# Decoder layer on one core: four PSUM banks for the maximum pass and two for the transposed scores, in place of three and three

## The chip, the core and the metric

The kernel runs on one core of a Trainium2 chip. The metric is the device time of one execution in microseconds (us), lower is better. "Before" is the kernel as it stands, "after" the changed one; both compute the same output.

## What is computed

One decoder layer on x of shape (2, 2048, 512): causal self-attention with 16 heads of 32, cross-attention to a context of 77 rows, and a mixture of 8 experts of which each token uses 2, each followed by a residual addition and a layer norm. The change lies in the causal self-attention alone:

```python
qkv = x @ Wqkv.T
q, k, v = jnp.split(qkv, 3, axis=-1)          # 16 heads of 32
dots = jnp.einsum('bhid,bhjd->bhij', q, k) * scale
dots = jnp.where(causal_mask, -jnp.inf, dots)
attn = jax.nn.softmax(dots, axis=-1)
out = jnp.einsum('bhij,bhjd->bhid', attn, v)
...
x = _layernorm(x + _L0_attn_ref(x, ...))
```

## The kernel before

There are three stages in order of time: projections (`project`), self-attention (`self_attention`), and everything behind it (`second_half`). The self-attention works through 8 groups (2 batches, 4 groups of 4 heads). A group has 4 chunks c of 512 query positions. Chunk c is worked through in 4(c+1) key tiles kt of 128 positions, so a group has 40 tiles; a tile has one unit for each of the 4 heads, so there are 160 units in a group and 1280 in all (`VU`). The tiles with kt < 4c have the full 512 columns; the last four of a chunk lie on the diagonal and have 512, 384, 256 and 128 columns. Of the 40 tiles, 24 are full and 16 diagonal. In this text "tile 29" is the 29th of a group, counted from 0.

Each score is computed twice, in two streams that share TensorE:

- The **transposed scores** `st_ps`, one unit at a time (`scores`, L865, and L868 for the mask on the diagonal). ScalarE takes a unit's exponential into `probs` (L762). TensorE multiplies the probabilities with the values (`values`, L885, into the bank `o_ps`), four steps behind the tile's last unit. The row sums come from GpSimd, which adds tiles up in `total` (L637), and at every third full tile from TensorE (`sums`, L899, into the bank `den_ps`), six steps behind.
- The **maximum pass**, scores the other way round, `s_ps` (`aux`, L851), from which VectorE takes row maxima (L804 for full blocks, L807 and L808 for blocks with the diagonal). It runs ahead of the other stream, 160 blocks and 4 small transposes (kind "rows", L843, read at L745 and L797) for a group. The list `DONE` spreads them over the 160 steps.

The order of instructions on each engine is written out by `step(i, s, ...)`: TensorE's step s issues the transposed score of unit s, then one block of the maximum pass, then `values` if a tile is due (the fourth step of each tile), then `sums` (the second step of a tile), then `totals` of a finished chunk, then further blocks of the maximum pass if the step has more than one. Each engine goes through its own list in order and waits on semaphores.

PSUM has eight banks of 512 float32 per partition. The attention stage holds one each for `o_ps` and `den_ps` and divides the other six between the two streams. A unit's bank is `p % RING`, and before its matmul TensorE waits until the exponential of the unit RING before it is done:

```python
pe.wait_ge(exp_done.sem, exp_done.at(i, before(p, RING, 2 * NVU)))     # scores, transposed
...
pe.wait_ge(s_read.sem, s_read.at(i, before(n, RING, 2 * NAUX)))        # maximum pass
```

ScalarE has other work in its list, placed by steps: the eviction of `o_ps` (`o_raw`, L768) behind the first exponential of the second tile after a chunk, that of `den_ps` (L772) two tiles later, and the conversion `o_out` (L777) of a tile that GpSimd has scaled (`o_sb`, L647), 46 steps after the chunk.

Of the kernel before, what the change touches and what calls it, by code (L numbers as in the profile page):

```python
# [5 lines left out]
F32, F16, BF16 = mybir.dt.float32, mybir.dt.float16, mybir.dt.bfloat16  # L6
# [7 lines left out]
P = 128  # L14
# [3 lines left out]
CH = 512  # L18
NC = N // CH
CPB = T // CH  # L20
# [45 lines left out]
def stored_at(n):  # L66

    return 16 * n + 1
# [333 lines left out]
def self_attention(nc, S, x_rows, q_parts, k_parts, v_rows, o_parts, inv_rows):  # L402
# [23 lines left out]
    NKU, NVU, NAUX = len(KU), len(VU), len(AUX)  # L426
# [3 lines left out]
              for c in range(CPB)]  # L430
    ADDS = [n for tiles in POOLED for n in tiles[1:]]
    NP = 5
    RING = 3

    VALUES, SUMS = 4, 6
    TOTALS = 12
# [59 lines left out]
    def before(n, ring, per):  # L496

        k = n % per
        return n - ring if k >= ring else n - k - 1 - (per - 1 - k) % ring
# [18 lines left out]
    def unit_at(s, lag, first, end):  # L518

        p = s - lag  # L520
        return None if (first is not None and p < first) or (end is not None and p >= end) else p
# [13 lines left out]
    def aux_at(s, first, end):  # L535

        if first is not None:
            reached = [AHEAD + (done_by(TAIL) - AHEAD) * n // TAIL for n in (s, s + 1)]
        else:
            reached = done_by(s), done_by(s + 1)  # L540
        return [n for n in range(*reached) if end is None or n < 2 * NAUX]

    with ExitStack() as stack:
        sb = lambda *a: stack.enter_context(nc.sbuf_tensor(*a))
        ps = lambda *a: stack.enter_context(nc.psum_tensor(*a))
# [19 lines left out]
        o_sb = sb("o_sb", [P, CH], F32)  # L565
        o_out = sb("o_out", [P, 2, 2, CH], F16)
        st_ps = ps("st_ps", [P, RING, CH], F32)
        s_ps = ps("s_ps", [P, RING, CH], F32)
        o_ps = ps("o_ps", [P, CH], F32)
        den_ps = ps("den_ps", [P, CH], F32)  # L570
        made, const_ready, factors_ready = (stack.enter_context(nc.semaphore(s)) for s in
# [14 lines left out]
        s_read = Count(nc, stack, "s_read", 2 * NAUX)  # L586
# [144 lines left out]
        @block.scalar  # L731
        def _(act):
            exp_done.lead(act)
            o_taken.lead(act)
            den_taken.lead(act)
            o_hi_done.lead(act)
            upper_ready.lead(act)

            def upper(i, n):

                k = n // NAUX * CPB + AUX[n % NAUX][1]
                slot = n % (2 * NAUX) % RING
                act.wait_ge(s_ready.sem, s_ready.at(i, n))
                act.wait_ge(rows_moved[k % 2], stored_at(2 * (CPB * i + k // 2)))
                nc.scalar.activation(max_rows[:, k % 2, 0], s_ps[0:HG * TT, slot, 0:P], ACT.Copy,  # L745
                                     scale=-1.0 / QK).then_inc(upper_ready.sem, 1)

            def step(i, s, first, end):
                for n in aux_at(s, first, end):
                    if AUX[n % NAUX][0] == "rows":  # L750
                        upper(i, n)
                p = unit_at(s, 0, first, end)
                if p is not None:
                    c, kt, h = VU[p % NVU]
                    off = max(kt - c * TT, 0) * P
                    k = p // HG
                    act.wait_ge(st_ready.sem, st_ready.at(i, p))
                    if h == 0:

                        act.wait_ge(pv_done.sem, pv_done.at(i, k - NP))  # L760
                        act.wait_ge(added.sem, added.at(i, adds_upto(k - NP) - 1))
                    nc.scalar.activation(probs[:, k % NP, h, off:], st_ps[:, p % (2 * NVU) % RING, off:], ACT.Exp,  # L762
                                         scale=SCALE).then_inc(exp_done.sem, 1)
                c = chunk_at(s, TAKEN[0], first, end)
                if c is not None:
                    act.wait_ge(pv_done.sem, pv_done.at(i, c // CPB * NKU + LAST_TILE[c % CPB]))
                    act.wait_ge(scaled.sem, scaled.at(i, c - 2))
                    nc.scalar.activation(o_raw[:, c % 2], o_ps[:], ACT.Copy).then_inc(o_taken.sem, 1)  # L768
                c = chunk_at(s, TAKEN[1], first, end)
                if c is not None:  # L770
                    act.wait_ge(den_ready.sem, den_ready.at(i, c))
                    nc.scalar.activation(den[:, c % 2], den_ps[:], ACT.Copy, scale=1.0 / XS).then_inc(den_taken.sem, 1)  # L772
                c = chunk_at(s, UPPER, first, end)
                if c is not None:
                    act.wait_ge(scaled.sem, scaled.at(i, c))
                    act.wait_ge(o_stored[c % 2], stored_at(CPB * i + c // 2))
                    nc.scalar.activation(o_out[:, c % 2, 0], o_sb[:], ACT.Copy).then_inc(o_hi_done.sem, 1)  # L777

            for n in range(AHEAD):
                if AUX[n][0] == "rows":  # L780
                    upper(0, n)
            laps(act, step)

        @block.vector
        def _(dve):
            for count in (s_read, max_ready, recips):
                count.lead(dve)

            def aux(i, n):
                what, c, unit = AUX[n % NAUX]  # L790
                slot = n % (2 * NAUX) % RING
                k = n // NAUX * CPB + c
                dve.wait_ge(s_ready.sem, s_ready.at(i, n))
                if what == "rows":

                    dve.wait_ge(upper_ready.sem, upper_ready.at(i, k))
                    nc.vector.scalar_tensor_tensor(max_rows[:, k % 2, 1], s_ps[0:HG * TT, slot, 0:P], -1.0 / QK,  # L797
                                                   max_rows[:, k % 2, 0], ALU.mult,
                                                   ALU.subtract).then_inc(s_read.sem, 1)
                    return  # L800
                j, h, s = unit
                highest = seg_max[:, k % 2, h, j, s:s + 1]
                if s < c:
                    nc.vector.reduce_max(highest, s_ps[:, slot], AX.X).then_inc(s_read.sem, 1)  # L804
                else:
                    width = (j + 1) * P
                    nc.vector.memset(ticked[:, j * HG + h:j * HG + h + 1], 0.0)  # L807
                    nc.vector.tensor_tensor_reduce(s_ps[:, slot, 0:width], s_ps[:, slot, 0:width],  # L808
                                                   later[:, CH - width:CH], 1.0, MASKED, ALU.add, ALU.max,
                                                   highest).then_inc(s_read.sem, 1)  # L810
                if n % NAUX == LAST_MAX[c]:

                    dve.wait_ge(s_read.sem, s_read.at(i, n))
                    nc.vector.reduce_max(row_max[:], seg_max[:, k % 2, :, :, 0:c + 1], AX.X).then_inc(max_ready.sem, 1)

            def step(i, s, first, end):
                for n in aux_at(s, first, end):
                    aux(i, n)
                c = chunk_at(s, INVERTED, first, end)
                if c is not None:  # L820
                    dve.wait_ge(den_moved[c % 2], 16 * (CPB * i + c // 2 + 1))
                    nc.vector.reciprocal(inv_small[:, c % 2], inv_small[:, c % 2]).then_inc(recips.sem, 1)

            dve.wait_ge(made, 7)
            for n in range(AHEAD):
                aux(0, n)
            laps(dve, step)

        @block.tensor
        def _(pe):  # L830
# [3 lines left out]
            def aux(i, n):  # L834
                what, c, unit = AUX[n % NAUX]
                k = n // NAUX * CPB + c
                slot, a = n % (2 * NAUX) % RING, k // CPB % 2

                pe.wait_ge(s_read.sem, s_read.at(i, before(n, RING, 2 * NAUX)))
                if what == "rows":  # L840

                    pe.wait_ge(max_ready.sem, max_ready.at(i, k))
                    nc.tensor.transpose(s_ps[0:HG * TT, slot, 0:P], row_max[:].rearrange("p h j -> p (h j)"),  # L843
                                        ident_f[:]).then_inc(s_ready.sem, 1)
                    return
                j, h, s = unit
                if j == h == s == 0:

                    pe.wait_ge(qk_loaded[a][c], 6 * 16 * (i + k // (2 * CPB) + 1))
                width = CH if s < c else (j + 1) * P  # L850
                nc.tensor.matmul(s_ps[:, slot, 0:width], q_pair[a][0:NR, c, h, j * P:(j + 1) * P],  # L851
                                 k_pair[a][0:NR, h, s * CH:s * CH + width], start=True,
                                 stop=True).then_inc(s_ready.sem, 1)
# [78 lines left out]
            for n in range(AHEAD):  # L932
                aux(0, n)
# [670 lines left out]
```

## Time and profile before

| | |
|---|---|
| runs | 2633.06, 2633.9, 2635.76 us, median 2633.9 us |
| the profiled execution | 2630.97 us, its span 2629.2 us, mean granted clock 0.958 |
| busy over the span | TensorE 2430.0 us (92%), VectorE 1715.9 (65%), ScalarE 1097.3 (42%), GpSimd 1119.8 (43%) |
| attention stage | first transposed score at 303.9 us, last at 1333.2 us |

The page divides the span into 40 slices of 66 us; the attention stage is the fifth to the twentieth. A matmul's row shows its whole way through the array (0.38 us at 512 columns), and the next one can begin 0.22 us behind it. "Idle before" of weight loads (PEld) counts time in which matmuls run, so it is more than TensorE loses.

### The profile page before, as it was taken

Reading aid. Unit: us, or ns where it says so; the run is one execution under the profiler, and the core shown is the slowest. Engines: PE = TensorE matmul, PEld = TensorE weight load, DVE = VectorE, ACT = ScalarE, POOL = GpSimd, SP = SyncE. Lnnn points to the kernel's source line nnn. Section 1 sums busy time; section 2 is a strip of 40 time slices with the busy share of each in tenths; the row PEclk is TensorE's granted clock in tenths of the full one; section 3 lists DMA queues with packets and bytes.
Section 4 is the critical chain, followed back from the end, with each engine's and each line's share of the span. In section 5 each row is a group of like instructions: output and inputs, shape, how many; then the busy total and the mean of one; then the engine's idle time right before and its main releaser. Section 6 shows DMA issues by size and latency. Waiting matters only on the chain. (4 is left out here: it accounts for less than half of the span.)

```text
span 2629.2 us, 42902 instructions
## 1 busy us (share of the span) xinstructions
PE 2430.0 (92%) x13556; PEld 1018.3 (39%) x13556; DVE 1715.9 (65%) x3957; ACT 1097.3 (42%) x2066; POOL 1119.8 (43%) x404
## 2 busy tenths in 40 slices
PE   8999799999999999999956799999999999999998
PEld 3444223332333233323213354444445454454543
DVE  4443687776777677767405477767677776767665
ACT  4331256665666566666623242332324232322420
POOL 0000379988898989898952111102111111101100
PEclk9999799999999999999977899999999999999999
DMA  7864312212121212140021101010100101010000
GB/s 250 294 212 156 89 38 54 58 42 59 42 58 42 63 38 76 28 111 20 25 93 60 45 1 62 1 46 18 41 22 1 63 1 46 17 45 17 1 17 17
DMA packets 130506, 155.66 MB, mean 59 GB/s; under 512 B 19838, under 2 KB 98174, under 8 KB 129245
## 3 DMA queue, kind: packets, MB, share of 16 engines
q1 hardware_dynamic: 130269, 152.69, 18.9%
q8 instruction: 126, 2.06, 0.3%
q14 instruction: 111, 0.91, 0.1%
HBM read 99.96 MB, written 52.17 MB: 58 GB/s over the span
## 5 line engine op out<-in xcount | busy, mean ns | idle before, releaser
L762 ACT ACTIVATE probs<-st_ps 128x512 f32<-128x512 f32 (+3 forms) x1280 | 605.3, 536 | 359.0 <-PE st_ps L865 206.6
L637 POOL TENSOR_TENSOR total<-total,probs 128x2048 f32<-128x2048 f32 (+3 forms) x200 | 706.3, 3531 | 77.8 <-ACT probs L762 65.6
L804 DVE TENSOR_REDUCE seg_max<-s_ps 128x1 f32<-128x512 f32 x768 | 506.2, 684 | 143.4 <-PE s_ps L851 139.9
L865 PE MATMUL st_ps<-q_pair,k_pair 98*128 98x512 f16 (+3 forms) x1280 | 445.5, 362 | 36.6 <-ACT probs L762 22.7
L851 PE MATMUL s_ps<-k_pair,q_pair 96*128 96x512 f16 (+3 forms) x1280 | 446.0, 363 | 31.9 <-DMA q_pair<-q_parts 11.2
L1429 PE MATMUL fps<-x2T,w_p_hi 128*128 128x512 f16 x1024 | 317.3, 379 | 0.0
L885 PE MATMUL o_ps<-probs,v_sb 128*32 128x512 f32 (+3 forms) x2560 | 309.0, 556 | 0.0
L808 DVE CUSTOM_DVE_ANT_0 s_ps<-s_ps,later 128x384 f32<-128x384 f32 (+3 forms) x512 | 250.4, 497 | 89.1 <-issue 85.9
L1429 PE MATMUL fps<-w_p_hi,hT 128*128 128x512 f16 x1024 | 306.1, 381 | 0.0
L865 PEld LDWEIGHTS st_ps<-q_pair,k_pair 98*128 98x128 f16 x1280 | 124.8, 99 | 357.7 <-ACT probs L762 264.7
L1133 POOL TENSOR_TENSOR rstd<-rstd,keep_power 128x4 f32<-128x4 f32 x24 | 26.1, 1090 | 552.0 <-DVE rstd L1254 552.0
L1148 POOL TENSOR_TENSOR soft<-soft,ssum 128x1232 f32<-128x1232 f32 x32 | 72.9, 2287 | 384.4 <-DVE ssum L1284 384.4
L851 PEld LDWEIGHTS s_ps<-k_pair,q_pair 96*128 96x128 f16 x1280 | 126.9, 100 | 227.3 <-DVE seg_max L804 111.4
L1216 ACT ACTIVATE hidden<-fps,keep_b_sb 128x512 f32<-128x512 f32 x128 | 86.4, 686 | 303.7 <-PE fps L1429 303.4
L1391 DVE SCALAR_TENSOR_TENSOR x<-fps,gates_un,x 128x512 f32<-128x512 f32 x256 | 183.9, 745 | 36.2 <-PE fps L1429 33.8
L1429 PE MATMUL fps<-w_p_lo,hT 128*128 128x512 f16 x512 | 194.6, 380 | 0.0
L1429 PE MATMUL fps<-x2T,w_p_lo 128*128 128x512 f16 x512 | 194.0, 379 | 0.0
L637 POOL TENSOR_TENSOR total<-probs 128x2048 f32<-128x2048 f32 (+1 forms) x32 | 136.4, 4263 | 52.8 <-ACT probs L762 52.8
L1380 DVE TENSOR_SCALAR hT<-hidden 128x512 f16<-128x512 f32 x128 | 86.0, 672 | 107.6 <-ACT hidden L1216 107.0
L1429 PEld LDWEIGHTS fps<-x2T,w_p_hi 128*128 128x128 f16 x1024 | 100.2, 98 | 128.8 <-DVE x L1391 5.9
L1429 PEld LDWEIGHTS fps<-w_p_hi,hT 128*128 128x128 f16 x1024 | 98.1, 98 | 131.0 <-issue 20.8
L1187 ACT ACTIVATE soft<-soft 128x1232 f32<-128x1232 f32 x32 | 39.4, 1231 | 200.4 <-DVE soft L1277 200.4
(164 smaller groups left out, 3403.8 us busy)
## 6 DMA issues: line engine op xcount, KB each, us to landing
k_pair<-k_parts SPq DMA_DIRECT2D x96, 128.0 KB, 3.6
q_pair<-q_parts SPq DMA_DIRECT2D x96, 128.0 KB, 4.7
x_raw<-xT_in SPq DMA_DIRECT2D x8, 1024.0 KB, 6.3
q_parts<-qk_out SPq DMA_DIRECT2D x32, 256.0 KB, 3.6
k_parts<-qk_out SPq DMA_DIRECT2D x32, 256.0 KB, 3.9
piece_raw<-w_in SPq DMA_DIRECT2D x8, 1024.0 KB, 8.7
v_rows<-v_out SPq DMA_DIRECT2D x32, 256.0 KB, 2.2
w_parts<-piece_cut SPq DMA_DIRECT2D x8, 1024.0 KB, 5.6
```

What stands on the lines that cost most here:

```text
L637: last = nc.gpsimd.tensor_tensor(summed[:, :, off:], other[:, :, off:], probs[:, k % NP, :, off:], ALU.add)
L762: nc.scalar.activation(probs[:, k % NP, h, off:], st_ps[:, p % (2 * NVU) % RING, off:], ACT.Exp, scale=SCALE).then_inc(exp_done.sem, 1)
L804: nc.vector.reduce_max(highest, s_ps[:, slot], AX.X).then_inc(s_read.sem, 1)
L808: nc.vector.tensor_tensor_reduce(s_ps[:, slot, 0:width], s_ps[:, slot, 0:width], later[:, CH - width:CH], 1.0, MASKED, ALU.add, ALU.max, h ...
L851: nc.tensor.matmul(s_ps[:, slot, 0:width], q_pair[a][0:NR, c, h, j * P:(j + 1) * P], k_pair[a][0:NR, h, s * CH:s * CH + width], start=True ...
L865: last = nc.tensor.matmul(st_ps[:, slot, off:], k_pair[a][:, h, kt * P:(kt + 1) * P], q_pair[a][:, c, h, off:], start=True, stop=not diagonal)
L885: last = nc.tensor.matmul(o_ps[out, off:], v_sb[a][:, kt, out], probs[:, k % NP, h, off:], start=(kt == 0), stop=final)
L1148: nc.gpsimd.tensor_tensor(soft[:, j], soft[:, j], ssum[:, j, :].rearrange("p (h a) -> p h a", a=1).broadcast_to([P, H, S2]), ALU.mult).the ...
L1216: nc.scalar.activation(hidden[:, n % 2], fps[:, (u * NUNIT + f) % FB], ACT.Gelu, bias=W["b1_sb"][:, n:n + 1], scale=UN).then_inc(gelu_done ...
L1380: nc.vector.tensor_scalar(hT[:, 0, e % 2, j], hidden[:, n % 2], XS, None, ALU.mult).then_inc(h_hi.sem, 1)
L1391: nc.vector.scalar_tensor_tensor(x2[q][:, j], bank, gates_un[q][:, j, e:e + 1], x2[q][:, j], ALU.mult, ALU.add).then_inc(added.sem, 1)
L1429: last = nc.tensor.matmul(bank, lhs(a, t), rhs(b, t), start=(n == 0), stop=(n == len(steps) - 1))
```

## The change

One constant becomes two. `RING`, now 2, is the number of `st_ps` banks; `S_RING`, 4, that of `s_ps` banks. The two waits, the bank of each write and the bank of each read follow them.

```diff
--- before.py
+++ after.py
@@ -430,7 +430,7 @@
               for c in range(CPB)]
     ADDS = [n for tiles in POOLED for n in tiles[1:]]
     NP = 5
-    RING = 3
+    RING, S_RING = 2, 4
 
     VALUES, SUMS = 4, 6
     TOTALS = 12
@@ -565,7 +565,7 @@
         o_sb = sb("o_sb", [P, CH], F32)
         o_out = sb("o_out", [P, 2, 2, CH], F16)
         st_ps = ps("st_ps", [P, RING, CH], F32)
-        s_ps = ps("s_ps", [P, RING, CH], F32)
+        s_ps = ps("s_ps", [P, S_RING, CH], F32)
         o_ps = ps("o_ps", [P, CH], F32)
         den_ps = ps("den_ps", [P, CH], F32)
         made, const_ready, factors_ready = (stack.enter_context(nc.semaphore(s)) for s in
@@ -739,7 +739,7 @@
             def upper(i, n):
 
                 k = n // NAUX * CPB + AUX[n % NAUX][1]
-                slot = n % (2 * NAUX) % RING
+                slot = n % (2 * NAUX) % S_RING
                 act.wait_ge(s_ready.sem, s_ready.at(i, n))
                 act.wait_ge(rows_moved[k % 2], stored_at(2 * (CPB * i + k // 2)))
                 nc.scalar.activation(max_rows[:, k % 2, 0], s_ps[0:HG * TT, slot, 0:P], ACT.Copy,
@@ -788,7 +788,7 @@
 
             def aux(i, n):
                 what, c, unit = AUX[n % NAUX]
-                slot = n % (2 * NAUX) % RING
+                slot = n % (2 * NAUX) % S_RING
                 k = n // NAUX * CPB + c
                 dve.wait_ge(s_ready.sem, s_ready.at(i, n))
                 if what == "rows":
@@ -834,9 +834,9 @@
             def aux(i, n):
                 what, c, unit = AUX[n % NAUX]
                 k = n // NAUX * CPB + c
-                slot, a = n % (2 * NAUX) % RING, k // CPB % 2
-
-                pe.wait_ge(s_read.sem, s_read.at(i, before(n, RING, 2 * NAUX)))
+                slot, a = n % (2 * NAUX) % S_RING, k // CPB % 2
+
+                pe.wait_ge(s_read.sem, s_read.at(i, before(n, S_RING, 2 * NAUX)))
                 if what == "rows":
 
                     pe.wait_ge(max_ready.sem, max_ready.at(i, k))
```

No engine's list changes: each of the five engines has the same instructions in the same order before and after, and the same semaphores to wait for. What changes is the value that two waits of TensorE ask for and the bank that each instruction names.

## Rows read from the trace of the kernel before

**Rows 1.** Stretch view, attention stage: us, engine busy (instructions), TensorE clock, DMA share, GB/s.
```profile
304.00:1334.00 1030.00, 976.56 (x6330) 315.12 (x6330) 730.34 (x2324) 645.86 (x1404) 906.85 (x299) 0.97 0.19 48
```

**Rows 2.** Page, costliest groups: busy, mean ns | idle before, releaser.
```profile
L851 PE MATMUL s_ps<-k_pair,q_pair 96*128 96x512 f16 (+3 forms) x1280 | 446.0, 363 | 31.9 <-DMA q_pair<-q_parts 11.2
```

**Rows 3.** Waits between 304 and 1334 us: total us, times, longest us.
```profile
PEld st_ps L865 <- ACT probs L762: 264.7, 388, 4.7
...
DVE seg_max L804 <- PE s_ps L851: 139.9, 186, 2.1
...
PEld s_ps L851 <- DVE seg_max L804: 108.6, 207, 2.2
...
ACT o_out L777 <- POOL o_sb L647: 28.4, 16, 5.1
```

**Rows 4.** Timeline of a full-width tile: start us, us, engine, line, operation.
```profile
800.25 0.38 PE L865 MATMUL st_ps<-q_pair,k_pair 98*128 98x512 f16 x1
...
800.82 2.06 ACT L762 ACTIVATE probs<-st_ps 128x512 f32<-128x512 f32 x4 [1.04 <-PE st_ps L865]
...
801.08 0.38 PE L865 MATMUL st_ps<-q_pair,k_pair 98*128 98x512 f16 x1
...
801.47 0.10 PEld L865 LDWEIGHTS st_ps<-q_pair,k_pair 98*128 98x128 f16 x1 [0.30 <-ACT probs L762]
...
801.51 0.38 PE L865 MATMUL st_ps<-q_pair,k_pair 98*128 98x512 f16 x1
...
801.99 1.06 PE L885 MATMUL o_ps<-probs,v_sb 128*32 128x512 f32 x8
...
802.99 0.39 PE L865 MATMUL st_ps<-q_pair,k_pair 98*128 98x512 f16 x1
```

**Rows 5.** Timeline of a tile whose steps hold row sums.
```profile
806.24 0.39 PE L865 MATMUL st_ps<-q_pair,k_pair 98*128 98x512 f16 x1
...
806.80 1.09 ACT L762 ACTIVATE probs<-st_ps 128x512 f32<-128x512 f32 x2 [1.19 <-PE st_ps L865]
...
807.22 1.06 PE L899 MATMUL den_ps<-probs,ones 128*32 128x512 f32 x8
...
808.22 0.39 PE L865 MATMUL st_ps<-q_pair,k_pair 98*128 98x512 f16 x1
```

**Rows 6.** Timeline of a tile with an eviction on ScalarE.
```profile
720.39 0.39 PE L865 MATMUL st_ps<-q_pair,k_pair 98*128 98x512 f16 x1
...
721.46 0.59 ACT L768 ACTIVATE o_raw<-o_ps 128x512 f32<-128x512 f32 x1
...
721.71 0.38 PE L865 MATMUL st_ps<-q_pair,k_pair 98*128 98x512 f16 x1
721.94 1.59 ACT L762 ACTIVATE probs<-st_ps 128x512 f32<-128x512 f32 x3
...
723.33 0.39 PE L865 MATMUL st_ps<-q_pair,k_pair 98*128 98x512 f16 x1
```

**Rows 7.** Timeline of a diagonal tile, 256 columns wide.
```profile
830.47 0.28 PE L865 MATMUL st_ps<-q_pair,k_pair 98*128 98x256 f16 x1
...
831.00 1.21 ACT L762 ACTIVATE probs<-st_ps 128x256 f32<-128x256 f32 x4 [1.10 <-PE st_ps L868]
...
831.44 0.28 PE L865 MATMUL st_ps<-q_pair,k_pair 98*128 98x256 f16 x1
...
832.50 0.23 PE L865 MATMUL st_ps<-q_pair,k_pair 98*128 98x128 f16 x1
```

**Rows 8.** Timeline where ScalarE waits for GpSimd.
```profile
908.58 1.26 POOL L647 TENSOR_TENSOR o_sb<-o_raw,inv 128x512 f32<-128x512 f32 x1
...
909.87 0.63 ACT L777 ACTIVATE o_out<-o_sb 128x512 f16<-128x512 f32 x1 [2.96 <-POOL o_sb L647]
...
910.72 0.39 PE L865 MATMUL st_ps<-q_pair,k_pair 98*128 98x512 f16 x1 [2.41 <-ACT probs L762]
```

**Rows 9.** Stretch view just behind it, columns as in rows 1.
```profile
913.00:918.00 5.00, 5.00 (x17) 1.25 (x15) 3.81 (x16) 2.75 (x5) 4.84 (x4) 0.50 0.00 0
```

## Prediction

> **What bounds the kernel now.** I first took the stretch view to see what limits the attention stage, the only stage that the change touches. In 1030 us TensorE has matmuls in flight for 976.56 us, GpSimd is busy for 906.85, VectorE for 730.34 and ScalarE for 645.86 [rows 1]. So TensorE's list sets the pace, with GpSimd about 120 us behind it. What matters for this change is what stops TensorE's list. The view of waits shows two waits on its weight loads: for ScalarE's exponential (264.7 us, 388 times) and for VectorE's maximum (108.6 us, 207 times) [rows 3]. These overstate the loss, since a weight load that stands idle behind `values` is covered by matmuls still running. That is why I went on to the timeline, tile by tile. The change gives the second wait more room (four banks) and takes room from the first (two banks).
>
> In the timeline of a full tile [rows 4] the reader should see how the ring of three works. The four exponentials start at 800.82 and take 2.06 us together; one of them is 0.60 us, so they start (2.06 - 0.60)/3 = 0.49 us apart. The first ends at 801.42, and at 801.47 the weight load of the tile's fourth score begins: 0.05 us from an exponential's end to the load that waited for it. The third score (801.08) did not wait, since the unit three before it was in the tile before. The `values` matmuls start at 801.99, 0.48 us behind the fourth score, and the next tile's first score comes 1.00 us behind them, at 802.99. The tile lasts 2.74 us.
>
> **The change part by part.** No instruction is added, removed or moved, so the whole effect is in two waits.
>
> *Two banks for transposed scores, a full tile.* The third score now waits for the first exponential: 801.42 + 0.05 = 801.47 in place of 801.08. The fourth waits for the second, which starts at 801.31 and ends at 801.91: it can start at 801.96 in place of 801.51 [rows 4]. Everything behind it, `values` included, moves by 0.45 us. TensorE's next scores don't win it back: ScalarE runs dry during `values` (it had stood idle 1.04 us before 800.82 in this same tile), because with two banks nothing more can be laid up for it. By the same steps I went through the 40 tiles of the group that begins at 708 us. Eight full tiles are of this kind; where VectorE had already held the list up, the loss is smaller (0.1 to 0.5), and I take 0.35 as their mean: 8 x 0.35 = 2.8 us.
>
> *Diagonal tiles.* The four exponentials of 256 columns start at 831.00, 0.38 us each and (1.21 - 0.38)/3 = 0.28 apart; the fourth score stands at 831.44, again 0.05 behind the first one's end [rows 7]. Now the third score goes at 831.43 and the fourth, after the third's mask and a block of the maximum pass, at about 831.77: +0.33 us on a tile of 2.03. Twelve tiles of a group are like it: 12 x 0.3 = 3.6 us.
>
> *Tiles with an eviction on ScalarE.* With `o_raw` behind the first exponential (721.46), the second starts only at 721.94 and ends at 722.54 (the three take 1.59). The fourth score, at 721.71 with three banks, has to wait until 722.59, +0.88 us [rows 6]; of that about 0.1 only replaces waits for VectorE in that tile. Six tiles of a group have `o_raw` or `den` there; three lose about 0.8 and three, where VectorE had held TensorE longer, about 0.35: 6 x 0.58 = 3.5 us.
>
> *Tiles with row sums.* `sums` stands between the second and the third score (807.22), and the third comes at 808.22, when both exponentials (806.80, 1.09 together, so over at 807.89) are done [rows 5]. Two banks are enough here: nothing, in 7 tiles. The last 7 of the 40 are tiles that already wait as long for VectorE or for other reasons (five or six blocks of the maximum pass, or the slow clock below): nothing either, and 7 + 7 + 8 + 12 + 6 = 40.
>
> That is 2.8 + 3.6 + 3.5 = 9.9 us in a group, and 79 us in 8 groups.
>
> *Four banks for the maximum pass.* The most it could give is every wait for VectorE, 108.6 us [rows 3], but that is mostly under running matmuls. What is left at the matmuls themselves is small: TensorE stood without any matmul for 31.9 us before maximum scores, and 11.2 of this is a load ahead of the stage [rows 2], so 20.7 at the least and 108.6 at the most. In the tiles above the longer wait for ScalarE has taken the place of the wait for VectorE already, which is how I costed them. For the rest I take 1 us a group, -8 us, near the lower bound. VectorE waits 139.9 us for scores [rows 3]; it isn't the bound, so shortening that gives nothing by itself.
>
> *What is late next, and what comes back.* GpSimd's list doesn't depend on the rings. It is behind once in most groups: `o_sb` ends at 909.84, ScalarE has waited 2.96 us for it with all exponentials queued behind `o_out`, and TensorE stood still for 2.41 us [rows 8]. Over the stage ScalarE waits 28.4 us so [rows 3]. TensorE reaches this place about 1.2 us later now (the tiles since GpSimd last ran dry), so that much of the wait is gone: about 1.2 x 7 = 9 us back.
>
> The sum is 79 - 8 - 9 = +62 us. Against the profiled execution (2630.97 us) that is 2693, and since the median of the runs is 2.9 us above it, **2696 us**.
>
> Here the Trainium skill bears on the other half of the change. "Perfetto Trace Analysis", section "Matmuls", says that independent matmul groups should rotate through different PSUM banks, so that the eviction of one overlaps the next group's matmuls. By that rule alone both streams lose or gain a bank alike and the sum would be near 0, the rival of no effect below. Rows 4 and rows 6 speak against reading it so: a bank is worth 0.45 and 0.88 us to the stream whose reader has just run dry, and the total stays at six.
>
> **The rivals.**
>
> *Absorbed.* TensorE's pauses fall where it would have waited anyway. The case for it: the maximum pass waits 108.6 us, and GpSimd is 88% busy, so delays before its late tiles are free. The slow clock belongs to it too: behind the pause of 2.41 us the granted clock was 0.50 from 913 to 918 us, with 17 matmul rows in 5 us [rows 8, 9], which costs about 2.5 us of work. If the pause shrinks and the clock then stays up, 7 x 2.5 = 17 us come back on top, and with the diagonal tiles at half my price (-14 us) and 10 us more from VectorE's waits the change is +21 us: 2655.
>
> *Worse than summed.* The tiles that I costed at nothing also lose 0.3 us (7 x 0.3 x 8 = 17 us), nothing comes back from GpSimd or VectorE (17 us), and pauses bring the clock down once more in each group (8 x 2.5 = 20 us): 62 + 54 = 116 us, 2750. For the clock, the trace shows the stage at 0.97 now [rows 1] with one clear fall behind a long pause [rows 8, 9]; new pauses would be of 0.4 to 0.9 us. "TensorE: Matmul & The Clock Gate", section "A second HAM failure mode: psum-queue depth-cycling", describes a kernel whose short idles while cycling through banks made the clock oscillate between its two levels. No row here shows that yet, and by that rule the last 20 us are due.
>
> *Faster.* The maximum pass is what really holds the list, through VectorE, and the exponentials catch up. The mechanism is the fourth `s_ps` bank: TensorE, no longer stopped at a block of the maximum pass, reaches the next transposed score earlier. It wins if it returns more than 79 us of the 108.6. Against it is that the fourth score already starts 0.05 us behind an exponential in rows 4 and rows 7: arriving earlier there is of no use. If all 108.6 came back: 2634 - 30 = 2604.
>
> *No effect.* The order of the lists hides both waits; this needs the third score never to arrive before the first exponential's end, and rows 4, 6 and 7 show it 0.39 us and more early.
>
> **How the numbers follow.** The summed case has a chance of 0.60 and a range of its own of 2670 to 2722 (each class's mean off by a third, 26 us). Absorbed 0.17, worse 0.15, faster 0.04, no effect 0.04. The range of 2655 to 2748 takes in the absorbed case down to its worked-out time and the worse one nearly whole. Some 0.2% (5 us) is about what a measurement of this kernel can tell from no change. Slower by more: 0.60 + 0.17 + 0.15 = 0.92, within: 0.04, faster: 0.04.
>
> **What would show it.** In the changed kernel's timeline the third and the fourth score of a full tile start 0.05 us behind the end of the first and the second exponential, and the tile of rows 4 lasts about 3.2 us; the tile of rows 6 about 3.7; the tile of rows 7 about 2.35; the distance in rows 5 from first to third score stays at 1.98. Waits of `st_ps` loads for ScalarE rise by some 60 to 100 us, those of `s_ps` loads for VectorE fall by more than half, GpSimd's idle time grows by as much as the stage, ScalarE's wait for `o_sb` shrinks, and the stages before 300 us and after the attention keep their lengths. I am wrong if VectorE's maxima turn out to hold TensorE at the places where I saw ScalarE (then tiles without an eviction keep their length), or if the granted clock of the stage moves away from 0.97 by more than 0.01 either way.

## The result

The changed kernel takes 2674.66 us (median of four runs, 2671.27 to 2678.38); the kernel before, on the same chip, 2633.48 us. The ratio is 1.0155, 95% interval [1.014, 1.017]: 41 us slower. The prediction was 2696 us, in a range of 2655 to 2748, so the direction and the range held and the sum of +62 us was 21 us too high.

All of it lies in the attention stage. The first transposed score starts at 304.04 us (before 303.95) and the last tile's exponentials are over at 1378.5 (before 1333.8), so the stage is 44.6 us longer; behind it the span is 3.3 us shorter, which was not forecast and which I did not follow, and in all it grew by 41.4.

Two rows of the page's costliest groups, after (busy, mean ns | idle before, releaser); of before, [rows 2] answers to the second, and the first stood at 36.6 us, 22.7 of them for ScalarE:

```profile
L865 PE MATMUL st_ps<-q_pair,k_pair 98*128 98x512 f16 (+3 forms) x1280 | 451.0, 360 | 85.4 <-ACT probs L762 63.8
L851 PE MATMUL s_ps<-k_pair,q_pair 96*128 96x512 f16 (+3 forms) x1280 | 432.6, 358 | 14.7 <-DMA q_pair<-q_parts 10.6
```

TensorE now stands without any matmul for 85.4 us before transposed scores, 49 more, and 41 of the 49 are listed as waits for exponentials (63.8 against 22.7). Before maximum scores it is 14.7 us in place of 31.9. The waits of the stage, after (us in total, times, longest), against [rows 3], show the same trade, and show ScalarE's wait for GpSimd at less than half:

```profile
PEld st_ps L865 <- ACT probs L762: 432.9, 716, 1.6
...
DVE seg_max L804 <- PE s_ps L851: 177.3, 232, 1.9
...
PEld s_ps L851 <- DVE seg_max L804: 43.5, 73, 0.8
...
ACT o_out L777 <- POOL o_sb L647: 11.2, 8, 2.2
```

The stretch view of the stage, after (us, busy of TensorE, weight loads, VectorE, ScalarE and GpSimd, clock, DMA share, GB/s), against [rows 1]:

```profile
304.00:1375.00 1071.00, 987.05 (x6291) 305.31 (x6292) 738.25 (x2324) 667.36 (x1396) 906.80 (x298) 0.98 0.18 46
```

The window is 41 us longer, GpSimd is busy in it for as long as before (906.80 against 906.85; the last 3.5 us of the stage lie behind the window), and the clock rose from 0.97 to 0.98.

The full tile of [rows 4], after, in the timeline:

```profile
815.71 0.38 PE L865 MATMUL st_ps<-q_pair,k_pair 98*128 98x512 f16 x1
...
816.28 2.17 ACT L762 ACTIVATE probs<-st_ps 128x512 f32<-128x512 f32 x4 [1.04 <-PE st_ps L865]
...
816.93 0.39 PE L865 MATMUL st_ps<-q_pair,k_pair 98*128 98x512 f16 x1 [0.24 <-ACT probs L762]
...
817.42 0.39 PE L865 MATMUL st_ps<-q_pair,k_pair 98*128 98x512 f16 x1
...
817.90 1.07 PE L885 MATMUL o_ps<-probs,v_sb 128*32 128x512 f32 x8
...
818.90 0.39 PE L865 MATMUL st_ps<-q_pair,k_pair 98*128 98x512 f16 x1
```

The exponentials take 2.17 us in place of 2.06. The first ends 0.60 behind 816.28, at 816.88, and the third score starts at 816.93. The fourth is at 817.42, 1.71 behind the tile's start where it had been 1.26. The tile lasts 3.19 us (2.74 before); about 3.2 was forecast. The tile with an eviction, against [rows 6]:

```profile
733.88 0.39 PE L865 MATMUL st_ps<-q_pair,k_pair 98*128 98x512 f16 x1
...
734.95 0.59 ACT L768 ACTIVATE o_raw<-o_ps 128x512 f32<-128x512 f32 x1
...
735.42 1.68 ACT L762 ACTIVATE probs<-st_ps 128x512 f32<-128x512 f32 x3
...
736.08 0.39 PE L865 MATMUL st_ps<-q_pair,k_pair 98*128 98x512 f16 x1 [0.37 <-ACT probs L762]
...
737.62 0.39 PE L865 MATMUL st_ps<-q_pair,k_pair 98*128 98x512 f16 x1
```

The second exponential starts at 735.42, ends at 736.02, and the fourth score follows at 736.08, 2.20 behind the tile's start (1.32 before). The tile lasts 3.74 us against 2.94; about 3.7 was forecast. The diagonal tile, against [rows 7]:

```profile
847.13 0.28 PE L865 MATMUL st_ps<-q_pair,k_pair 98*128 98x256 f16 x1
...
848.10 0.28 PE L865 MATMUL st_ps<-q_pair,k_pair 98*128 98x256 f16 x1 [0.24 <-ACT probs L762]
...
848.44 0.27 PE L865 MATMUL st_ps<-q_pair,k_pair 98*128 98x256 f16 x1
...
849.49 0.23 PE L865 MATMUL st_ps<-q_pair,k_pair 98*128 98x128 f16 x1
```

It lasts 2.36 us against 2.03; 2.35 was forecast. The tile of [rows 5], with row sums, has its third score 1.97 us behind its first, as before.

Lengths of tiles are distances between the first transposed scores of neighbouring tiles. By the classes of the prediction, the sums over a group's tiles (medians of the second, fourth and sixth group) are:

| class | tiles | forecast, us a group | after less before | the same with `o_out` later in both (below) |
|---|---|---|---|---|
| full, waits for exponentials | 8 | +2.8 | +2.55 | +2.66 |
| diagonal | 12 | +3.6 | +5.28 | +3.25 |
| eviction behind the first exponential | 6 | +3.5 | +3.56 | +3.57 |
| row sums | 7 | 0 | 0.0 | 0.0 |
| rest | 7 | 0 | -5.28 | +0.24 |
| sum | 40 | +9.9 | +6.1 | +9.72 |

The last two rows of classes show where the forecast and the result part: tiles 24 and 25 became 3.04 and 1.68 us shorter and are in the rest; 1.28 us of the diagonal class is tile 23, in which ScalarE's pause now falls. The three together are 3.4 us shorter. Here is that place in the fourth group, after, against [rows 8], which are of the fifth: GpSimd's `o_sb`, ScalarE's `o_out` behind it, and the first score of tile 24.

```profile
795.38 1.27 POOL L647 TENSOR_TENSOR o_sb<-o_raw,inv 128x512 f32<-128x512 f32 x1
...
796.68 0.63 ACT L777 ACTIVATE o_out<-o_sb 128x512 f16<-128x512 f32 x1 [1.22 <-POOL o_sb L647]
...
797.53 0.39 PE L865 MATMUL st_ps<-q_pair,k_pair 98*128 98x512 f16 x1 [1.04 <-ACT probs L762]
```

ScalarE waits 1.22 us where it had waited 2.96, TensorE stands still for 1.04 in place of 2.41, and the clock does not fall behind it in this group. The stretch view of the 5 us that follow, against [rows 9] (17 matmul rows at clock 0.50):

```profile
798.00:803.00 5.00, 4.20 (x25) 1.35 (x22) 4.92 (x27) 4.33 (x9) 4.84 (x3) 1.00 0.39 87
```

### The profile page after: what moved, and what is told of

Same layout as the page of the kernel before. It is cut to its first block and busy times, and to the rows that moved or that the text cites. A ratio compares the mean times of both kernels' runs of the same rounds, so it can differ in the third digit from the quotient of the medians.

```text
span 2670.6 us, 42902 instructions
## 1 busy us (share of the span) xinstructions
PE 2443.5 (91%) x13556; PEld 1009.7 (38%) x13556; DVE 1723.9 (65%) x3957; ACT 1121.5 (42%) x2066; POOL 1120.1 (42%) x404
## 3 DMA queue, kind: packets, MB, share of 16 engines
q8 instruction: 126, 2.06, 0.3%
## 5 line engine op out<-in xcount | busy, mean ns | idle before, releaser
L762 ACT ACTIVATE probs<-st_ps 128x512 f32<-128x512 f32 (+3 forms) x1280 | 628.4, 532 | 396.8 <-PE st_ps L865 227.8
L804 DVE TENSOR_REDUCE seg_max<-s_ps 128x1 f32<-128x512 f32 x768 | 510.2, 687 | 181.7 <-PE s_ps L851 177.3
L865 PE MATMUL st_ps<-q_pair,k_pair 98*128 98x512 f16 (+3 forms) x1280 | 451.0, 360 | 85.4 <-ACT probs L762 63.8
L851 PE MATMUL s_ps<-k_pair,q_pair 96*128 96x512 f16 (+3 forms) x1280 | 432.6, 358 | 14.7 <-DMA q_pair<-q_parts 10.6
L1429 PEld LDWEIGHTS fps<-w_p_hi,hT 128*128 128x128 f16 x1024 | 98.0, 98 | 131.0 <-issue 20.8
```

The source lines that it names most:

```text
L865: last = nc.tensor.matmul(st_ps[:, slot, off:], k_pair[a][:, h, kt * P:(kt + 1) * P], q_pair[a][:, c, h, off:], start=True, stop=not diagonal)
L1429: last = nc.tensor.matmul(bank, lhs(a, t), rhs(b, t), start=(n == 0), stop=(n == len(steps) - 1))
```

## Experiments

Each kernel ran beside the kernel before. Medians of that one lay between 2633.16 and 2634.5 us. All kernels compute the whole output. Two accounts of the missing 21 us were open: **A**, GpSimd's lateness and the slow clock behind it gave back more than the 9 us allowed for; **B**, the fourth bank of the maximum pass gave back more than 8 us.

### The loss alone: two banks and three

```diff
-    RING, S_RING = 2, 4
+    RING, S_RING = 2, 3
```

> RING 2, S_RING 3: the change with its gain part left out, one PSUM bank unused. The cost of two banks for the transposed scores alone. The prediction was +62 us and +41 was measured; this says which credit was too small. Theory A (GpSimd and clock): the fourth bank of the maximum pass gives back next to nothing (8 us or less), and the missing 20 us come from the pause behind o_sb and the slow clock after it, which this kernel loses as well: 2672 to 2685. Theory B (VectorE): the fourth bank gives back 20 us or more, since waits for VectorE are 108.6 us before and 43.5 after: 2695 or more.

Measured: 2683.22 us (2682.12 to 2683.41), ratio 1.0183 [1.0166, 1.02]. The fourth bank of the maximum pass is worth 8.6 us, the size that the prediction gave it. Account B falls. What the bank does for the waits is plain (us in total, times, longest, this kernel; with four banks it is 43.5 us in 73 times), but those waits are mostly under running matmuls or beside the wait for ScalarE. What TensorE's matmuls themselves stood still before maximum scores in the stage is 11.3 us here and 3.2 with four banks, a difference of 8 us, as large as the price of the bank:

```profile
PEld s_ps L851 <- DVE seg_max L804: 71.2, 130, 0.8
```

### The maximum pass with two banks

```diff
-    RING, S_RING = 2, 4
+    RING, S_RING = 3, 2
```

> RING 3, S_RING 2: the maximum pass alone loses a bank. With two banks TensorE may run only one block ahead of VectorE. If VectorE was not far from binding with three (TensorE's loads waited 0.05 us behind a maximum's end some 320 of 1312 times in the kernel before), this costs as much as the loss on the other side or more: theory A 2700 to 2790. If the maximum pass has room to spare, as a rival has it: 2640 or less.

Measured: 2706.38 us (2702.78 to 2720.04), ratio 1.0263 [1.0245, 1.028], +72 us. The trace is of the slowest of the five executions (2720.04 us). The loads' wait for VectorE doubles against [rows 3], and now matmuls stand still for it too, 51.4 us in place of 9.5:

```profile
PEld s_ps L851 <- DVE seg_max L804: 221.0, 372, 1.2
...
PE s_ps L851 <- DVE seg_max L804: 51.4, 142, 0.6
```

So neither stream can spare its third bank: it is worth some 49 us to the transposed scores (two and three against three and three) and 72 to the maximum pass. The 49 are what is left after GpSimd's wait and the clock gave something back: with `o_out` later in both kernels (below) the same pair stands 71 us apart, 2669.27 against 2598.09. For the maximum pass no such pair was run.

### The change turned round: four and two

```diff
-    RING, S_RING = 2, 4
+    RING, S_RING = 4, 2
```

> RING 4, S_RING 2: the change turned round. Its difference to the kernel with three and two is what a fourth bank of transposed scores is worth. Theory A: the fourth score of a tile waits for the first exponential no more (some 170 waits, 29 us in all at the most), so 10 to 30 us below the run with three and two, and still above the kernel before, 2680 to 2770. Rival (the transposed scores are what is short of banks, the maximum pass isn't): below 2633.

Measured: 2708.74 us (2705.2 to 2709.57), ratio 1.0275 [1.0258, 1.0293]. The expected gain of 10 us at the least against three and two is not there: 2.4 us the other way, inside the intervals. TensorE's weight loads wait 221.6 us for VectorE, as with three and two, and a fourth bank of transposed scores finds nothing to shorten:

```profile
PEld s_ps L851 <- DVE seg_max L804: 221.6, 376, 1.2
...
PE s_ps L851 <- DVE seg_max L804: 54.0, 146, 0.6
```

### Evictions one step later, two and four banks

In ScalarE's list the evictions go behind the second exponential of a tile in place of the first.

```diff
-    TAKEN = VALUES + 1, TOTALS + 1
-    DEN_MOVED = TAKEN[1] + 1
+    TAKEN = VALUES + 2, TOTALS + 2
+    DEN_MOVED = TOTALS + 2
```

> The changed kernel with the evictions of o_ps and den_ps one step later in ScalarE's list, behind the second exponential of the tile in place of the first. By the prediction's third class the fourth score waits for the second exponential, which no longer has the eviction (0.49 us) ahead of it: the tiles 1, 5, 7, 13, 15, 25, 27 of a group lose 0.45 us each less, and the diagonal ones like them: 7 x 0.45 x 8 = 25 us less, 2650 (2645 to 2660). Rival (the eviction's time is due wherever it stands, since ScalarE has to do it before the next tile's exponentials): 2670 to 2680.

Measured: 2661.67 us (2656.88 to 2663.12), ratio 1.0097 [1.008, 1.0114]: 13 us less than the change, half of the 25 that were expected, and just outside the range of 2645 to 2660. Groups 2, 4 and 6 (counted from 1) shortened by 3.4, 2.3 and 3.4 us, groups 3 and 5 by 0.1 each. The timeline where tile 24 of the fourth group begins says why: `o_out`, then the first and the third score of tile 24, and the first of tile 25.

```profile
791.14 0.63 ACT L777 ACTIVATE o_out<-o_sb 128x512 f16<-128x512 f32 x1 [1.71 <-POOL o_sb L647]
...
792.00 0.58 PE L865 MATMUL st_ps<-q_pair,k_pair 98*128 98x512 f16 x1 [1.53 <-ACT probs L762]
...
792.79 0.63 PE L865 MATMUL st_ps<-q_pair,k_pair 98*128 98x512 f16 x1
...
795.83 0.38 PE L865 MATMUL st_ps<-q_pair,k_pair 98*128 98x512 f16 x1
```

With the tiles ahead of it shorter, TensorE's list arrives earlier, ScalarE waits longer for GpSimd (1.71 us against 1.22), TensorE stands still for 1.53 us (1.04), and its next matmuls run at 0.63 us in place of 0.38. Tile 24 takes 3.83 us where the changed kernel has 2.73. In groups 3 and 5 the same happened, with longer slow stretches. The stretch view of 3 us of it, columns as before:

```profile
793.00:796.00 3.00, 3.00 (x16) 0.92 (x15) 2.56 (x14) 2.15 (x4) 2.92 (x2) 0.59 0.37 103
```

### The same edit with three banks, a control

The two lines of the last diff, on the kernel before.

> The kernel before (three and three) with the two evictions one step later in ScalarE's list. A control for the eviction run. With three banks the fourth score waits for the first exponential, and the eviction stands behind that one in either place, so theory A says within 6 us of 2634. Rival (the eviction belongs one step later for any ring): 10 us or more faster, as it was with two banks (13 us).

Measured: 2636.64 us (2631.44 to 2638.52, ten runs), ratio 1.0013 [1.0003, 1.0022]. With three banks the eviction may stand in either place. Its price belongs to the ring of two.

### `o_out` four steps later, with three and three

```diff
-    UPPER = SCALED + 8
+    UPPER = SCALED + 12
```

> The kernel before with o_out four steps later in ScalarE's list, so that ScalarE need not stand still for GpSimd's o_sb. If the pause (2.41 us of TensorE) and the slow clock behind it are what made tiles 24 and 25 of most groups 5.4 and 5.3 us long where the changed kernel has 2.7 and 3.7, then these shorten to about 2.7 and 3.1 also with three banks: 5 us a group less, 7 groups, 25 to 35 us less: 2600 to 2610. Rival (GpSimd, 88% busy in the stage, is the bound there and the wait moves to another instruction, or the clock falls anyway): 2625 or more.

Measured: 2598.09 us (2593.71 to 2601.08), ratio 0.987 [0.9853, 0.9886]: 35 us less than the kernel before, the fastest of all. The constant moves more than `o_out`: the low half of the output, its store and the turn of the loop (`LOWER`, `STORED`, `TAIL`) are counted from it and move along by the same four steps. Where ScalarE had stood still for 2.96 us, with TensorE in tile 24 [rows 8], it doesn't now; this is the same place in the fourth group (the last score of tile 23, the first of 24, `o_sb`, `o_out`, and the first of 25 and 26):

```profile
762.25 0.23 PE L865 MATMUL st_ps<-q_pair,k_pair 98*128 98x128 f16 x1
...
764.41 0.39 PE L865 MATMUL st_ps<-q_pair,k_pair 98*128 98x512 f16 x1 [1.20 <-DMA q_pair<-max_rows]
...
764.53 1.27 POOL L647 TENSOR_TENSOR o_sb<-o_raw,inv 128x512 f32<-128x512 f32 x1
...
765.96 0.63 ACT L777 ACTIVATE o_out<-o_sb 128x512 f16<-128x512 f32 x1
...
766.68 0.38 PE L865 MATMUL st_ps<-q_pair,k_pair 98*128 98x512 f16 x1
...
769.91 0.39 PE L865 MATMUL st_ps<-q_pair,k_pair 98*128 98x512 f16 x1
```

Tile 24 lasts 2.27 us and tile 25 3.23, where before it was 5.78 and 5.42 in this group; tile 23 grew from 1.71 to 2.97, by the wait for the transfer that the second of these rows shows. `o_out` no longer waits, since `o_sb` ended at 765.80. Not all of the 35 us is this place. By groups the traces give 5.4, 5.7, 5.8, 4.4, 4.3 and 2.9 us for the first six, and 8.7 for the seventh, where another wait is gone: in the kernel before VectorE waited there for the transfer of the row sums, in tiles 18 and 30, 4.52 and 2.52 us, and TensorE with it, 3.61 and 1.69 us. The kernel before, tile 18 of the seventh group:

```profile
1143.91 0.25 DVE L822 RECIPROCAL inv_small<-inv_small 128x16 f32<-128x16 f32 x1 [4.52 <-DMA inv_small<-den]
...
1144.76 0.61 PE L851 MATMUL s_ps<-k_pair,q_pair 96*128 96x512 f16 x1 [3.61 <-DVE seg_max L808]
```

In this run VectorE has no such wait above 1 us in the seventh group. Why it is gone was not tested. The stage of this run, in the stretch view, and its clock:

```profile
304.00:1300.00 996.00, 954.97 (x6330) 310.83 (x6330) 725.25 (x2324) 644.70 (x1405) 906.82 (x298) 0.99 0.20 50
```

### `o_out` four steps later, with two and four

The same line, on the changed kernel.

> The changed kernel with o_out four steps later. ScalarE's wait for o_sb is 1.2 us a group there and no slow clock stands behind it in most groups: 6 to 12 us less, 2663 to 2669. Together with the same edit on the kernel before this gives the price of two banks with no credit from GpSimd and the clock: if that account is right the difference of the two is near the summed cost of 79 us less 8 for the fourth bank, 60 to 70 us. Rival (the credit is not from there): the difference stays at 41 us.

Measured: 2661.36 us (2659.28 to 2665.96), ratio 1.0115 [1.0098, 1.0132]: 13 us less than the change. The difference to the run before this one is 63 us, inside the 60 to 70 expected, and by tile 9.72 us a group (last column of the table). The stage, now at the same clock as with three banks:

```profile
304.00:1366.00 1062.00, 984.04 (x6330) 304.84 (x6330) 737.65 (x2324) 669.79 (x1405) 910.57 (x299) 0.99 0.18 47
```

### Both edits, with two and four

> The changed kernel with o_out four steps later and both evictions one step later. With the slow clock out of the way the eviction edit should give its whole price: three odd groups of the eviction run gained 3.4 us each and two others gained nothing because the clock fell once more there. So 8 x 3.4 = 27 us below the run with o_out later (2661): 2634, with 2630 to 2642 as the range. Rival (13 us is all that it is worth): 2648.

Measured: 2637.18 us (2632.59 to 2642.45, ten runs), ratio 1.0012 [1.0003, 1.0022]: 24 us less than with `o_out` alone. The tile of [rows 6] in this kernel: first score, eviction, first score of the next tile, 3.25 us apart (3.74 with the eviction one step earlier).

```profile
723.32 0.39 PE L865 MATMUL st_ps<-q_pair,k_pair 98*128 98x512 f16 x1
...
724.86 0.60 ACT L768 ACTIVATE o_raw<-o_ps 128x512 f32<-128x512 f32 x1
...
726.57 0.39 PE L865 MATMUL st_ps<-q_pair,k_pair 98*128 98x512 f16 x1
```

By the same comparison as in the table, six tiles with an eviction shortened by 0.48 or 0.49 us each, and two more (3 and 25) that I had counted elsewhere.

### Two and three with `o_out` later

> RING 2, S_RING 3 with o_out four steps later: what the fourth bank of the maximum pass is worth when neither the pause nor the slow clock is in the way. Theory A: the same 8 us as without the edit (2683 against 2675): 2666 to 2673. Rival (the fourth bank's credit was hidden by the clock): 2680 or more.

Measured: 2669.27 us (2667.49 to 2671.1), ratio 1.0133 [1.0116, 1.0149]. The fourth bank is worth 7.9 us here, and 8.6 without the edit. The clock did not hide anything of it.

### The maximum pass further ahead

The kernel before with `o_out` later and

```diff
-    READY = 6
+    READY = 9
```

> The kernel before with o_out four steps later (2598 us) and the maximum pass three steps further ahead (READY 9 in place of 6), which writes its blocks at other steps. In the trace of that kernel the first score of a long chunk waits up to 1.2 us for the transfer of the row maxima (q_pair<-max_rows) and the tile before it is 2.6 long where it had been 1.7. If that transfer is what is late next, it is 0.8 to 1.2 us a group: 2588 to 2594. Rival (blocks land in other tiles, where they make TensorE wait for VectorE as much as is gained): 2596 or more.

Measured: 2601.63 us (2598.66 to 2604.32), ratio 0.9877 [0.9861, 0.9894]. Nothing is gained against 2598.09. TensorE's wait for the transfer is nearly gone (0.6 us in place of 6.0), and tile 23 of the fourth group is down from 2.97 to 1.60 us. But tile 25 grew from 3.24 to 4.15, because TensorE's list now arrives earlier and ScalarE waits for GpSimd once more. The first score of tile 25, `o_out`, and the second score:

```profile
765.01 0.39 PE L865 MATMUL st_ps<-q_pair,k_pair 98*128 98x512 f16 x1
...
765.20 0.63 ACT L777 ACTIVATE o_out<-o_sb 128x512 f16<-128x512 f32 x1 [1.00 <-POOL o_sb L647]
...
766.37 0.39 PE L865 MATMUL st_ps<-q_pair,k_pair 98*128 98x512 f16 x1 [0.76 <-ACT probs L762]
```

Over the stage these waits of ScalarE rose from 3.7 to 9.4 us. Other tiles of this group grew or shrank as blocks of the maximum pass moved (tile 21 by +0.81 us, tile 22 by -0.65). The rival had the time right, but its mechanism is not shown: TensorE's matmuls waited as long for VectorE's maxima as without the edit (7.1 us for L804 in both).

## Why the prediction was right, and what was mis-sized

**The mechanism** was right in the tiles that were worked out, to 0.04 us or better: 3.19, 3.74, 2.36 us against 3.2, 3.7 and 2.35, and no change in tiles with row sums. The start of a score 0.05 us behind the end of an exponential, read in [rows 4] and [rows 7], carried the whole forecast. In the changed kernel's trace 518 of the 1280 loads of transposed scores start 0.050 to 0.055 us behind the exponential two units before, where 177 did so with three banks.

**The classes** were right in size: 9.9 us a group forecast, less 1 for the fourth bank, and 9.7 to 10.7 measured in the second to the sixth group once the pause behind `o_sb` is out of both kernels. Multiplying by 8 was not right: the first group lost only 2.6 us and the last two 7.0 and 6.5. So the two kernels stand 63 us apart where 79 - 8 = 71 was forecast. By the traces the 8 us less are three parts: 10.5 less in the first and the last two groups, 5.7 more in the five between them, and 3.3 less behind the stage. I had read the tiles of one group in the middle. What is different in the others I did not follow tile by tile, but for one thing: the fourth bank gives 3 of its 8 us in the first group, where it is 3.2 us longer with three banks.

**Four banks for the maximum pass, -8 us,** was right in sum: 8.6 and 7.9. The term was a choice of 1 us a group near the lower bound and not worked out by tiles, and 3 us of it fell to the first group alone, so that the sum met it is partly luck. That the recorded waits of its loads fell by more than half (108.6 to 43.5 us) is true as forecast too, and it shows how little such a number says: a weight load's wait under running matmuls costs nothing.

**"What is late next, and what comes back"**, -9 us, was the mis-sized term. It priced the shorter wait at GpSimd alone, at 1.2 us for 7 groups; the clock behind it was put at nothing in the sum and left to the "absorbed" rival. The pause was sized well: TensorE's pauses at the start of tile 24 (those above 0.9 us, in all eight groups) add up to 20.1 us in the kernel before and to 10.1 in the changed one. The clock was not: between the first score and the last exponential the granted clock stood at 0.50 for 71.9 us before and for 38.2 us after. Half of the difference, 17 us, is an estimate of what that can have given back.

The two pairs of runs give the whole term: putting `o_out` later is worth 35 us with three banks and 13 with two, so with two banks 22 us of it had already come back. That is 13 more than the 9, and with the 8 us of the paragraph on the classes it is the 21 missing (62 - 13 - 8 = 41, as measured). Of the 22 us, 20.8 lie in the first six groups by the traces, and there in the neighbourhood of tile 24 (tiles 23 to 25 are 3.4 us shorter in the table, with the clock at 1.00 where it had been 0.50). The seventh group is another matter: TensorE's waits behind VectorE and the transfer of the row sums, 3.61 and 1.69 us before, are absent after, with the clock falls behind them, so tiles 18 and 30 are 5.26 and 3.45 us shorter. The prediction has no term for that, and why the waits are gone was not tested.

That the shortened pause is what keeps the clock up is supported by the pauses of TensorE at the start of tile 24 in the first six groups: 2.2 to 3.0 us in the kernel before, all six with a slow stretch behind them; 1.5 to 1.6 in the run with later evictions, four of six with one; 1.0 to 1.1 in the changed kernel, none of six. It is no sure rule: in the last run two pauses of 2.4 and 2.5 us had no slow stretch behind them, and in the changed kernel a pause of 1.06 us at tile 4 of the first group had one of 3.4 us. No run changed the pause and nothing else.

**The case called absorbed** had the mechanism of what came back, the clock, with 17 us for it, and asked too much besides (diagonal tiles at half price, 10 us more from VectorE), and **worse than summed** failed on the clock: new pauses of 0.2 to 0.4 us in nearly every tile left the stage at 0.98, above the 0.97 of before. The failure that the Trainium skill tells of in "TensorE: Matmul & The Clock Gate", section "A second HAM failure mode: psum-queue depth-cycling", did not show in the changed kernel. With three and two it can't be ruled out: in the profiled execution, 14 us above that kernel's median, the granted clock stood at 0.50 from 322 to 342 us, and no pause of TensorE in that stretch was longer than 0.47 us. The advice of the Trainium skill in "Perfetto Trace Analysis", section "Matmuls", to rotate independent groups through banks, holds here with a measure: the third bank is worth 49 us (71 with `o_out` later) and 72 us to the two streams, the fourth nothing to the transposed scores and 8 us to the maximum pass.

**The test that I set** for being wrong, the clock of the stage moving away from 0.97 by more than 0.01, seems not to be met by the two digits of the view (0.97 and 0.98). From the times at 0.50 above the means are 0.965 and 0.982, so it moved by 0.017 and the test was met. It points at the same step as the runs: the clock that the sum left out.

## What to carry to other kernels

A ring of n banks decides which earlier read a matmul waits for. Take one tile of the timeline, add the reader's duration and the hand-over time (0.05 us here), and write down each start for n - 1: that gives the price of a bank before any run, and tells which tiles don't care. With a ring of two, an eviction ahead of the reader's second item cost 0.48 or 0.49 us in each of eight tiles of a group here, so try it one place on; that gave back 24 of the 63 us. Then look for the engine that is late once in a while: a wait of 3 us in ScalarE's list for an off-path result, once in most groups, and the slow clock behind it were most of the 35 us that four steps of slack gave back, nearly as much as the whole change. Such a wait can also hide what a change costs: it made two banks look 22 us cheaper than they are without it.

## What the runs showed of the hardware

At two places in the stage, at tile 13 of the third and of the fifth group, TensorE stands still for 3 us with no wait on any engine, where, as I infer below, the program's loop over pairs of groups goes round, and the clock falls behind it. The timeline of the changed kernel at the second of these, and the stretch view of the 8 us behind it:

```profile
894.88 0.39 PE L865 MATMUL st_ps<-q_pair,k_pair 98*128 98x512 f16 x1 [2.98 <-issue]
...
895.25 0.63 PE L865 MATMUL st_ps<-q_pair,k_pair 98*128 98x512 f16 x1
```

```profile
895.00:903.00 8.00, 8.00 (x29) 2.08 (x32) 4.67 (x12) 4.52 (x9) 6.51 (x3) 0.57 0.50 134
```

The kernel before has the same pause there (3.07 us). It belongs to no ring, and makes these two groups about 5 us longer than their neighbours (137.2 against 132.1 us after). I infer the turn of the loop from the place, since the loop's body begins at step 52, which is tile 13. The five runs with `o_out` later bear it out: their loop body begins at step 56, and the pauses, 2.3 to 3.0 us long, stand at tile 14 of the same two groups. No run took the loop away.
